# The skip term of a state-space layer: scaled on ACT and added by DVE, in place of diagonal matmuls on PE

## What is computed

```python
def step(state, inp):
    dA_t, dt_t, B_t, C_t, x_t = inp
    state = state * dA_t[:, :, None, None] + (dt_t[:, :, None] * x_t)[..., None] * B_t[:, None, None, :]
    y = jnp.einsum('bhpn,bn->bhp', state, C_t)
    return (state, y)
_, ys = jax.lax.scan(step, init, (tm(dA), tm(dt), tm(Bm), tm(Cm), tm(xs)))
y = jnp.moveaxis(ys, 0, 1) + Dp[None, None, :, None] * xs      # the skip
y = y.reshape(Bsz, L, D_INNER)
y = _rmsnorm(y * jax.nn.silu(z), gnorm_w, 1e-05)
return x + jnp.einsum('ble,de->bld', y, W_out)
```

## Time and profile before

| | value |
|---|---|
| median of 3 runs | 1182.82 us (1180.0 to 1187.27) |
| the profiled execution | 1189.9 us |
| its span in the trace | 1188.1 us |
| attention, 0 to 392 us | 392 us |
| state-space scan, 392 to 907 us | 515 us |
| experts, 907 us to the end | 281 us |
| PE busy over the span | 949.8 us (80%) |
| DVE busy | 707.1 us (60%) |
| ACT busy | 548.1 us (46%) |
| POOL busy | 201.5 us (17%) |

### The profile page before, as it was taken

The page is one execution under the profiler, slowest core; times in us unless marked ns, Lnnn a source line. Parts: engine busy times, 40 slices in busy tenths (PEclk is TensorE's granted clock), DMA queues, the critical chain, the costliest instruction groups (busy, mean ns, idle before and its releaser), DMA issues.

```text
span 1188.1 us, 21166 instructions
## 1 busy us (share of the span) xinstructions
PE 949.8 (80%) x7630; PEld 738.0 (62%) x7630; DVE 707.1 (60%) x1846; ACT 548.1 (46%) x867; POOL 201.5 (17%) x186
## 2 busy tenths in 40 slices
PE   3689888998764778787676877777678999899888
PEld 2555555555443657675565656566567878777877
DVE  2865656555723464546446472646566887788875
ACT  1534444344335453455544444454532555555553
POOL 0000000000100505042230504124160111110100
PEclk9898889988875877898877888888887999999999
DMA  4300000000003020030301102030310000000000
GB/s 140 105 1 18 18 18 18 0 18 18 1 1 61 2 50 13 2 62 1 63 2 38 24 9 55 1 61 2 61 55 1 1 19 19 19 18 18 2 17 36
DMA packets 29602, 31.73 MB, mean 27 GB/s; under 512 B 4560, under 2 KB 24656, under 8 KB 29520
## 3 DMA queue, kind: packets, MB, share of 16 engines
q1 hardware_dynamic: 29520, 30.62, 10.7%
HBM read 17.24 MB, written 4.98 MB: 19 GB/s over the span
## 4 chain that ended last, share of the span: by engine, by line
PE 53%; DVE 24%; ACT 9%; issue 9%; POOL 2%; DMA 1%; SPq 1%; DVEq 0%; ACTq 0%; POOLq 0%
PE ps L662 5%; PE ps L991 5%; DVE cacc L1591 4%; PE ps L649 3%; PE ps L908 3%; DVE acc L1840 3%; PE ps L638 2%; PE ps L887 2%; PE ps L738 2%; PE ps L896 2%; PE ps L880 2%; PE ps L875 2%; PE ps L616 2%; PE ps L739 2%; PE ps L740 2%
## 5 line engine op out<-in xcount | busy, mean ns | idle before, releaser
L1840 DVE SCALAR_TENSOR_TENSOR acc<-ps,comb,acc 128x128 f32<-128x128 f32 x512 | 140.9, 344 | 25.8 <-PE ps L991 23.3
L991 PEld LDWEIGHTS ps<-w_f,hid 128*128 128x128 f32 x1024 | 131.4, 192 | 18.4 <-ACT hid L1328 8.2
L991 PE MATMUL ps<-w_f,hid 128*128 128x128 f32 x1024 | 137.4, 277 | 5.5 <-ACT hid L1328 4.7
L1259 ACT ACTIVATE dcy<-ps 128x1024 f32<-128x1024 f32 x64 | 65.9, 1029 | 160.3 <-PE ps L848 160.3
L1328 ACT ACTIVATE hid<-ps,b_f 128x512 f32<-128x512 f32 x128 | 86.3, 686 | 112.1 <-PE ps L740 111.8
L1662 DVE SCALAR_TENSOR_TENSOR dcy<-dcy,g_sb 128x1024 f32<-128x1024 f32 x64 | 84.7, 1323 | 69.5 <-ACT dcy L1259 69.4
L1463 DVE TENSOR_REDUCE nmax<-ps 128x1 f32<-128x1024 f32 x64 | 78.2, 1222 | 41.0 <-PE ps L621 40.8
L1591 DVE SCALAR_TENSOR_TENSOR cacc<-ps,cw,cacc 128x1023 f32<-128x1023 f32 (+5 forms) x72 | 92.0, 1278 | 13.4 <-ACT cacc L1198 11.7
L1118 ACT ACTIVATE pt<-ps 128x512 f32<-128x512 f32 x64 | 38.2, 597 | 116.1 <-PE ps L649 115.8
L1468 DVE COPY pt<-ps 128x512 f32<-128x512 f32 x64 | 44.1, 689 | 74.4 <-PE ps L649 74.2
L649 PEld LDWEIGHTS ps<-id_f,probs 128*128 128x128 f32 x512 | 65.2, 155 | 34.9 <-issue 22.3
(11 more groups left out here) (214 smaller groups left out, 1953.3 us busy)
## 6 DMA issues: line engine op xcount, KB each, us to landing
c_dec<-exp_dram SPq DMA_DIRECT2D x32, 256.0 KB, 5.2
X<-in_x SPq DMA_DIRECT2D x8, 512.0 KB, 3.4
q_b<-q_a SPq DMA_DIRECT2D x16, 256.0 KB, 2.9
c_rep<-cacc SPq DMA_DIRECT2D x32, 128.0 KB, 2.5
out<-o_ch SPq DMA_DIRECT2D x8, 512.0 KB, 2.6
w_f<-in_w SPq DMA_DIRECT2D x2, 512.0 KB, 4.0
cst_f<-in_sel_rows SPq DMA_DIRECT2D x1, 512.0 KB, 4.4
cst_f<-in_head_rows SPq DMA_DIRECT2D x1, 512.0 KB, 5.4
```

Source lines behind the costliest of these rows:

```text
L991: last = nc.tensor.matmul(ps[:, Y_BANKS[n], t * P:(t + 1) * P], hid[n % 2][:, t * P:(t + 1) * P], w2_f[:, e, :], start=True, stop=True)
L1840: done = nc.vector.scalar_tensor_tensor(acc[u][:, tt, :], ps[:, bank, t * P:(t + 1) * P], comb[u][:, tt, e:e + 1], acc[u][:, tt, :], ALU.m ...
```

## The change

The diagonal products on PE are gone, and with them `d_diag` and the two DVE operations that make it. The first group that then writes the PSUM bank opens it: L880's first four, or L887's at c = 0. ACT, in `gather_x`, multiplies each half of `cacc` by the column `d_col` in place, behind each gather, and signals `m_skip_ready`. DVE's one product per chunk becomes two operations: y (PSUM) plus the scaled `cacc` (SBUF) into `y_t`, then, after a wait for its own result, `y_t` times `zs` in place.

```diff
-                for g in range(2):
-                    nc.tensor.matmul(o[:, g, :], d_diag[:, g, :], cacc[u][:, g, t], start=(g == 0), stop=False,
-                                     skip_group_check=True)
                 if c >= 1:
+                    pe.sem_inc(wait_carrier, 1)
                     for h in range(NH):
                         r = slice(h % 4 * DS, h % 4 * DS + DS)
                         nc.tensor.matmul(o[r, h // 4, :], state[r, h // 4, :, c - 1], c_dec[u][r, c, h // 4, :],
-                                         start=False, stop=False, tile_position=(h % 4 * DS, h % 4 * DS),
+                                         start=(h in (0, 1, 2, 3)), stop=False, tile_position=(h % 4 * DS, h % 4 * DS),
                                          skip_group_check=True)
...
-                                            start=False, stop=True, tile_position=(0, h % 4 * HD),
+                                            start=(c == 0 and h < 4), stop=True, tile_position=(0, h % 4 * HD),
...
                                          ACT.Copy).then_inc(m_x_gathered, 1)
+                    nc.scalar.activation(cacc[u][:, g, :], cacc[u][:, g, :], ACT.Copy,
+                                         scale=d_col[:, g:g + 1]).then_inc(m_skip_ready, 1)
...
-                    nc.vector.tensor_scalar(d_diag[:, g, :], id_f[:], d_col[:, g:g + 1], None, ALU.mult)
...
+                    dve.wait_ge(m_skip_ready, 2 * b + 2)
+                    dve.sem_inc(wait_carrier, 1)
                     r = slice(c * P, (c + 1) * P)
                     nc.vector.tensor_tensor(y_t[:, :, r], ps[:, 6 + c % 2, 0:DI].rearrange("p (g t) -> p g t", g=2),
-                                            zs[u][:, :, r], ALU.mult).then_inc(m_gated_ready, 1)
+                                            cacc[u][:, 0:2, r], ALU.add).then_inc(m_skip_added, 1)
+                    dve.wait_ge(m_skip_added, NT * b + c + 1)
+                    nc.vector.tensor_tensor(y_t[:, :, r], y_t[:, :, r], zs[u][:, :, r],
+                                            ALU.mult).then_inc(m_gated_ready, 1)
```

More of the change, by code:

```diff
@@ L90, in hybrid_kernel @@
         d_col = sb("d_col", [P, 2])
-        d_diag = sb("d_diag", [P, 2, P])
         decf = sb("decf", [P, 2, DS, NT - 1])
@@ L318, in hybrid_kernel @@
         m_x_gathered = sem("m_x_gathered")
+        m_skip_ready = sem("m_skip_ready")
+        m_skip_added = sem("m_skip_added")
         m_inner_product = sem("m_inner_product")
@@ L869, in output_rows @@
                 o = ps[:, 6 + c % 2, 0:DI].rearrange("p (g t) -> p g t", g=2)
-                t = slice(c * P, (c + 1) * P)
                 if c == 1:
```

## The result

| | before | after |
|---|---|---|
| median | 1185.05 us (1180.0 to 1190.51, 4 runs) | 1202.24 us (1196.64 to 1205.47, 4 runs) |
| ratio, 95% interval | | 1.0139 [1.0077, 1.0201] |
| the profiled execution, its span | 1189.9, 1188.1 us | 1205.47, 1203.7 us |
| first product of the last picture's `out_product` in chunk 0 | 863.5 us | 873.6 us |
| experts begin (first ACT row of their hidden layer) | 916.1 us | 933.6 us |

The account below looks back on a forecast made before the run. PE was taken to lead the scan but idle in waits, the largest for DVE's softplus chain. Summed: -11.8 + 6.3 + 1.4 + 0.8 + 0.9 - 0.4 = -2.8 us against median 1182.82, giving 1180.0 us; range 1170 to 1192.

Parts of the forecast that it names:

- The sum: Whole kernel: PE's savings against added DVE, port and end costs, -2.8 us net, 1180.0 us; chance 0.65 within some 6 us.
- The first rival: `turn_b` to end of `inner_products`: PE falls to half clock, 3.9 us per picture; chance 0.08 for four pictures or more.
- the sign to look for: Scan stretch: a granted clock below 0.80 would show the slower rival, by TensorE's clock.
- The chain on DVE: y of chunk 3 to `cumulate`: two gates, each 0.45 us longer, move everything after them; 6.3 us in seven pictures.
- The 1.4 for the port: Chunk 3: the product's two SBUF inputs make it wait for POOL, 0.2 us more in each of seven pictures.
- The port at chunk 7: Product held by POOL's `c_dec` until 588.9, lengthened to 2 us, delaying `g_sb`; 0.8 us on the path.
- PE's saving: Diagonal products removed: 11.8 of 51.9 us come off the path, at chunks 3 (4.2), 5 (3.0), 6 (1.7) and 7 (2.9).
- Where the text had it at zero: Chunks 0, 1, 2 and 4: no PE saving, as PE waits there for ACT or DVE anyway.
- chunk 3's 0.6: Chunk 3: DVE idled until this y came, so the diagonal's 0.6 us counts in full, 4.2 in seven pictures.
- 0.7 for chunks 5 and 6: Behind `cumulate`: diagonals removed save 3.0 us at chunk 5 and 1.7 at chunk 6, over seven pictures.
- the 1.0 assumed: ACT: sixteen scales of 1024 columns, two per picture, at 1.0 us each, hidden with cover 0.4; cost taken as 0.
- The third rival: No saving at chunk 5 or 7 and ACT's cover gone, PE waiting before `inner_products`: +7.3 us, 1190.1; chance 0.09.

Follow-up runs that it names:

- e2: Kernel before without the diagonal products on PE and nothing in their place, skip term left out: 1195.43 us, 1.0109 of before.
- e4: Kernel after with two useless filler products on PE in each of chunks 5 to 7: 1180.67 us, 0.9962 of before.
- e5: Kernel after with two useless filler products on PE in each of chunks 0 to 4: 1219.39 us, 1.0268 of before.
- e16: Skip by both means: chunks 0 to 4 as in the kernel after, chunks 5 to 7 as in the kernel before: 1180.31 us, 0.9952 of before.
- e1: Kernel after with two useless products of the diagonals' size put back on PE in every chunk: 1203.65 us, 1.0192 of before.
- e6: Kernel after with filler products in two PE waits, 16 ahead of `cumulate` and 8 ahead of `turn_normed`: 1199.09 us, 1.0118 of before.
- e9: Kernel after with fillers ahead of `cumulate` (29), `turn_normed` (10), `turn_x` (8) and `turn_b` (4): 1192.90 us, 1.0060 of before.
- e7: Kernel before with filler products in two PE waits, 16 ahead of `cumulate` and 8 ahead of `turn_normed`: 1166.49 us, 0.9857 of before.
- e8: Kernel before with fillers ahead of `cumulate` (26), `turn_normed` (10), `turn_x` (8) and `turn_b` (2): 1169.94 us, 0.9880 of before.
- e17: e16 with 16 filler products ahead of `cumulate` and 8 ahead of `turn_normed`: 1193.22 us, 1.0042 of before, executions widely spread.
- e11: Kernel after with the addition written back to PSUM, so the product reads one SBUF tile: 1195.92 us, 1.0118 of before.
- e10: Kernel after without the sixteen scales on ACT, 1 in place of factor D: 1193.71 us, 1.0111 of before.

## Why the prediction was wrong, point by point

**The clock.** The step that failed is the price of taking PE's work away. The sum took a diagonal product for its 0.6 us and let everything around it keep its speed. Measured, the products' removal is +10.5 us (e2) where the text had -11.8. The first rival had the mechanism, the sign to look for (below 0.80; it was 0.71) and a fitting time (1195.6 from four pictures on), but a chance of 0.08 for that size. Its place was in part another: it priced `turn_b` to the end of `inner_products`, while `out_product`, right behind, has 10.8 of the 19.2 us that the three groups lost. "It happened in one picture of seven" was read as evidence for rarity. The rows of before had more: the earlier trace rows show half clock on the diagonal at 569.14, and the trace of before has `out_product` at full clock at 525.85 (32 products in 3.81 us, shown above) and at half at 596.23:

```profile
596.23 5.04 PE L908 MATMUL ps<-w_out,y_t 128*128 128x128 f32 x30
```

The row has 30 of the 32 products. It stands behind 5.2 us of issue at the loop's jump, shown further down, and the half-clock `out_product` at 731.36 behind 3.7; the one in the picture of the earlier trace rows, at 459.24, has no such gap ahead of it. My reading is that a kernel whose clock falls in some pictures and holds in others stands at an edge, and that there a small change of PE's work counts for more than its duration; the first half is in the rows, the second fits e2, e4 and e5 and isn't shown beyond them. What is shown is that, with chunks 0 to 4 left light, the work of chunks 5 to 7 holds the clock (e4 against after, e16), and that in chunks 0 to 4 the same work costs time. Why e1, with PE's work as before, does not get before's clock is not shown; beside the operands of the fillers the difference left is in the timing of DVE and ACT.

**Where the clock fell.** The Trainium skill describes the relapse after idle time ("TensorE: Matmul & The Clock Gate", section "HAM oscillation — how this bites in real kernels"). The traces agree for chunk 1, half clock behind 3.35 us of idle at 538.28, and it is still low at `turn_normed`, 1.97 us instead of before's 1.67. They show another case too: at 588.77 the clock is low though PE's only gap since `turn_x` (581.74) was the 1.03 us ahead of `turn_b`, and the groups between are mostly tiles of 32 rows or columns. Fillers in the two long waits (e6) did not prevent it, and fillers in four waits (e9) did not either.

**The chain on DVE.** Right in size. The addition and the product behind it are as foretold, as is the longer wait of `cumulate`:

```profile
555.21 0.62 POOL L505 TENSOR_TENSOR xdt<-xs,dts 128x256 f32<-128x256 f32 x1 [6.41 <-PE ps L885]
555.31 0.42 DVE L1721 TENSOR_TENSOR y_t<-ps,cacc 128x256 f32<-128x256 f32 x1 [2.66 <-PE ps L885]
555.77 0.42 DVE L1724 TENSOR_TENSOR y_t<-y_t,zs 128x256 f32<-128x256 f32 x1
```

The product starts 0.46 after the addition, against 0.45; PE then waits 7.49 us (text: some 7.5), where the earlier trace rows have 6.30; in the mean of seven pictures it is 7.3 against 6.6. The chain itself is measured best from DVE's first operation on the y of chunk 3 to `cumulate`: 13.2 to 13.3 us in each of the four traces with one operation a chunk (before, e2, e7, e8), 14.0 to 14.3 in each of the thirteen with two (e16 and e17 have two in chunks 3 and 4), whatever the clock. That is 1.0 us a picture, 7 in seven, where the sum had 6.3 + 1.4 = 7.7. The 1.4 for the port did not come as told: POOL's `xdt` ends at 555.83, the product begins at 555.77 and lasts its 0.42. That the total is near is in part luck. What came was another meeting on the port, with no term in the sum:

```profile
559.90 0.61 POOL L505 TENSOR_TENSOR xdt<-xs,dts 128x256 f32<-128x256 f32 x1 [4.08 <-PE ps L885]
559.94 0.66 DVE L1601 TENSOR_TENSOR dtr<-dtp 128x64 f32<-128x64 f32 x1
```

DVE's small operation at the head of the softplus chain lasts 0.66 us instead of its median 0.216, and ends 0.09 after POOL's `xdt`. The addition had moved DVE's chain onto POOL's start, in this picture; at 768.92 it lasts 0.32, in the other six of its eight its usual 0.22 (at 491.54 the one behind it is held instead).

**The port at chunk 7.** Right in kind, and shorter here than told, since DVE and POOL didn't start as I had placed them:

```profile
588.31 4.30 POOL L523 TENSOR_TENSOR c_dec<-c_dec,c_rep 128x896 f32<-128x896 f32 x2 [0.93 <-DMA c_rep<-cacc]
589.49 1.20 DVE L1724 TENSOR_TENSOR y_t<-y_t,zs 128x256 f32<-128x256 f32 x1
```

1.20 us instead of 0.42. Six pictures have such a product: three at 1.10 to 1.22 and three at 1.89 to 2.06, the length foretold. Over all 64 the product is 34.4 us busy, 7.2 above 64 times 0.425; in e11, with one SBUF input, nothing is above. The Trainium skill's rule, "SBUF — State Buffer", section "Who interferes with whom", fits these two meetings of DVE and POOL, and e11.

**PE's saving.** Where the text had it at zero it is zero: ahead of the state in chunk 1, have PE waiting 16.3 us in seven times; e2 has 18.7 and after 22.0, so the diagonal of chunk 0 went into that wait and the addition came on top, and `turn_in` to `turn_normed` stayed at 11.4 to 11.5 us. Of chunk 3's 0.6, 0.5 is there in e2 (from `turn_normed` to the y of chunk 3 12.8 before, 12.3 in e2) and 0.1 in the kernel after (12.6), where in the picture shown the products of chunks 1 and 2 run at half clock. Behind `cumulate` the stretch to `inner_products` shrank by 0.9 us a picture, where the sum had (3.0 + 1.7) / 7 = 0.7 for chunks 5 and 6; in e2 it shrank by 0.2 only. It was all lost again from `inner_products` to `turn_in`, by 1.8 us a picture, and by 7.4 in the last.

**ACT.** The pair of gathers is spread as told, and the scale is longer than the 1.0 assumed:

```profile
586.04 1.14 ACT L1231 ACTIVATE cacc<-cacc,d_col 128x1024 f32<-128x1024 f32 x1
587.08 1.01 ACT L1228 ACTIVATE xs<-ps 128x1024 f32<-128x1024 f32 x1
```

PE did not wait for the second gather: it ends at 588.09, `inner_products` starts at 588.77 without a wait. `turn_b` waited 1.03 (text: 1.1). The third rival did not come about. What the scales cost beyond that, e10 does not show.

**A term that was missing.** Where the hardware loop jumps back, PE has gaps of issue. First before, then after:

```profile
591.59 0.72 PE L848 MATMUL ps<-rhs_c,lhs_c 128*128 128x512 f32 x2 [2.83 <-issue]
592.16 0.17 PE L896 MATMUL ps<-ones_f,sqt 128*128 128x1 f32 x1
594.72 1.65 PE L896 MATMUL ps<-ones_f,sqt 128*128 128x1 f32 x7 [2.40 <-issue]
```
```profile
593.00 1.22 PE L849 MATMUL ps<-rhs_c,lhs_c 128*128 128x512 f32 x2 [0.45 <-issue]
```

5.2 us against 0.45. At the two jumps before has 5.2 and 3.7, after 0.45 and 1.7, e2 2.2 and none, e4 2.1 and 2.1. Of the seventeen traces only before and e1 (4.9 and 4.7), the two with products in the diagonals' place in all chunks and no fillers in the waits, have more than 2.3 us at a jump. This gave the changed kernel some 7 us that the sum did not have, and the clock took them too. It is part of why e4 and e16 come out below before though the sum says some 4 us above, and some 5 us of e7's 18 are of this kind (1.7 and 2.0 there). What makes the gap long or short was not tried.

## What to carry to other kernels

Where PE's rows show the same group at half clock in one repetition and at full in the next, work taken from PE is not worth its duration: first ask what the groups behind it cost at either clock (here 7.1 against 12.7 us), and weigh that against the saving (0.6 us a chunk). Before moving work off PE, try the cheap test of taking it out without replacement: if that is slower, the gain that you counted on isn't there, and where the work stands matters more than how much it is (e16, which moves only chunks 0 to 4, is 0.5% faster). And the mean clock of a stage is a sign, not a price (0.76 went with 1219 us, 0.71 with 1202), so decide by the times of the groups.

## What was not expected of the hardware

- Useless products at the right place made a kernel faster: 16 and 8 of them in PE's two waits 18 us (1166.49 against 1184.88), six a picture in chunks 5 to 7 21.6 us (1180.67 against 1202.24).
- The clock falls where PE had no gap above 1.03 us for 7 us, mostly among tiles of 32 rows or columns: at 588.77, 3.78 us instead of 2.05.
- A higher granted clock need not be a shorter time: e8 has 0.92 in the scan and 1169.94 us, e7 0.89 and 1166.49.
